# Rows of two expert layers turned inside their expert stages instead of in stages of their own

## The reference, cut to what matters

```
# L0: every token goes to its top 2 of 8 experts, each expert takes 512 rows per choice
xe = jnp.where(valid[..., None], xf[tok_idx], 0.0)
h  = jax.nn.gelu(jnp.einsum('ech,ehf->ecf', xe, w1), approximate=True)   # 256 -> 1024
ye = jnp.einsum('ecf,efh->ech', h, w2)                                   # 1024 -> 256
# L1: gated experts: silu(x @ w_gate) * (x @ w_up) @ w_down, 8 experts, inner width 352, top 2
```

## Time and profile before

| | us |
|---|---|
| median of 3 runs (3170.32 to 3171.92) | 3170.71 |
| the profiled execution, its own time | 3168.09 |
| its span, first to last instruction | 3166.2 |
| TensorE busy, 21348 matmuls | 2538.6 (80%) |
| VectorE busy | 2188.5 (69%) |
| ScalarE busy | 1274.6 (40%) |

### The profile page before, as it was taken

The page is one execution under the profiler, slowest core; times in us unless marked ns, Lnnn a source line. Parts: engine busy times, 40 slices in busy tenths (PEclk is TensorE's granted clock), DMA queues, the critical chain, the costliest instruction groups (busy, mean ns, idle before and its releaser), DMA issues. The chain is left out here.

```text
span 3166.2 us, 57355 instructions
## 1 busy us (share of the span) xinstructions
PE 2538.6 (80%) x21348; PEld 1656.4 (52%) x21348; DVE 2188.5 (69%) x5562; ACT 1274.6 (40%) x2273; POOL 990.4 (31%) x1412
## 2 busy tenths in 40 slices
PE   1998385999904497997989876886699999969982
PEld 1443263666604266886556543444466555656662
DVE  5997763666557764675678767997766545867757
ACT  1777353333202323111346654773222222256622
POOL 3442271110074260113656326871300000024330
PEclk9999598999956698998999997998799999979996
DMA  3331266221150147665721022100100000011001
GB/s 96 131 110 69 96 232 204 80 79 62 41 158 12 65 168 259 226 229 183 233 79 48 12 74 81 43 23 5 64 10 13 1 1 1 1 39 48 29 10 58
DMA packets 158167, 266.90 MB, mean 84 GB/s; under 512 B 22635, under 2 KB 106137, under 8 KB 151876
## 3 DMA queue, kind: packets, MB, share of 16 engines
q1 hardware_dynamic: 131204, 186.97, 17.8%
q0 software_dynamic: 17904, 76.23, 7.1%
q10 hardware_dynamic: 8784, 0.04, 0.2%
HBM read 175.25 MB, written 88.34 MB: 83 GB/s over the span
## 5 line engine op out<-in xcount | busy, mean ns | idle before, releaser
L1495 ACT ACTIVATE l2e_hf<-l2e_H 128x512 f32<-128x512 f32 x208 | 124.2, 597 | 381.4 <-PE l2e_H L1451 381.4
L1626 POOL TENSOR_TENSOR all_m_rstd<-all_m_sq,all_mhalf 128x8 f32<-128x8 f32 x24 | 39.6, 1648 | 557.4 <-DVE all_m_sq L1611 523.0
L772 DVE TENSOR_REDUCE l0a_mx<-l0a_S 128x2 f16<-128x512 f32 x256 | 168.0, 686 | 21.7 <-PE l0a_S L606 21.0
L1533 DVE CAST l2e_hh<-l2e_hf 128x512 f16<-128x512 f32 x208 | 92.7, 446 | 122.9 <-ACT l2e_hf L1495 108.6
L721 ACT ACTIVATE l0a_pf<-l0a_ST 128x512 f32<-128x512 f32 x256 | 146.6, 602 | 53.1 <-PE l0a_ST L620 52.9
L768 DVE CUSTOM_DVE_ANT_0 l2s_masked<-l2s_S,l2s_mq 128x128 f32<-128x128 f32 (+1 forms) x512 | 153.3, 349 | 20.4 <-PE l2s_S L606 19.9
L1451 PE MATMUL l2e_H<-l2o_hi,l2e_w 128*128 128x512 f16 x576 | 151.4, 381 | 15.8 <-DVE l2e_w L1509 15.8
L1495 ACT ACTIVATE l0e_hf<-l0e_H 128x512 f32<-128x512 f32 x128 | 76.4, 597 | 206.1 <-PE l0e_H L1451 206.1
L1451 PE MATMUL l2e_H<-l2e_hh,l2e_w 128*128 128x512 f16 x640 | 155.1, 379 | 0.0
L1535 DVE TENSOR_TENSOR l2e_hl<-l2e_hf,l2e_hh 128x512 f16<-128x512 f32 x208 | 147.3, 708 | 7.2
L1451 PE MATMUL l1e_H<-l1b_hi,l1e_w 128*128 128x256 f16 (+1 forms) x936 | 144.8, 274 | 7.8 <-DMA l1e_w<-packed,all_second_weight_row 7.8
(11 more groups left out here) (711 smaller groups left out, 7508.3 us busy)
## 6 DMA issues: line engine op xcount, KB each, us to landing
l0e_wf<-in_L_ffn_w SPq DMA_DIRECT2D x16, 1024.0 KB, 7.7
rows<-l0a_zeros SPq DMA_DIRECT2D x16, 640.0 KB, 5.9
l1u_rb<-rows SPq DMA_DIRECT2D x20, 512.0 KB, 5.0
results<-l1e_y SPq DMA_DIRECT2D x39, 256.0 KB, 3.4
l0a_kv<-in_ctx SPq DMA_DIRECT2D x16, 512.0 KB, 4.1
rows<-l0a_zeros SPq DMA_DIRECT2D x16, 512.0 KB, 4.9
l0d_p_cx<-in_ctx SPq DMA_DIRECT2D x16, 512.0 KB, 6.4
l0u_rb<-rows SPq DMA_DIRECT2D x16, 512.0 KB, 5.1
```

Of the source, the lines that this page charges most:

```text
L772: m = nc.vector.tensor_reduce(mx[h % 2][:, :, i], ps[:, :].rearrange("p (u k) -> p u k", u=TB), AX.X, ALU.max)
L1495: nc.scalar.activation(hf[q % 4][0:fn, :], pair_of(q, lay)[0][0:fn, :], lay.func, scale=1.0 / WS).then_inc(acted, 1)
L1533: nc.vector.tensor_copy(high, v).then_inc(hi_done, 1)
L1626: self.nc.gpsimd.tensor_tensor(out=(self.rstd, self.rstd2)[which][:, g], in0=(self.sq, self.sq2)[which][:, g], in1=self.g.mhalf[:, 0:self. ...
```

## The change

`turn_rows_stage` is gone, and so are `hi` and `lo` of all rows. `experts_stage` gets `raw=rows` and does the turning itself:

- SyncE loads a block of rows (512 rows in L0, 256 in L1) into a ring of 4 (L0) or 6 (L1) buffers `rb`. In L0 the loads stand around `load(n)`; in L1 six are issued first, and one behind each store.
- TensorE turns blocks 0 and 1 before the first unit. After up(a=1) it turns the next pair's first block, after down(a=0) the next pair's second. A turn is 16 transposes in L0 (two halves of 8) and 8 in L1.
- Both parts go into one of two PSUM banks `T`. ScalarE copies a half (128x1024 fp16) to `xT[b % 2]` by one instruction; VectorE copies nothing. The up unit waits for `copied`.
- The banks for `T` come from `Y`: in L0 four tiles now share two banks, so that a down tile waits for the copy 2 tiles back (`DEPTH` = 2). L1 had two `Y` banks before.

```diff
+    HALVES, BLKS = gt // 2, NE * tiles // gt
+    RING = 4 if packed is None else 6
+    DEPTH = gt if raw is None else 2
...
+            pairs = [st.ps(f"Y{i}") for i in range(2)]
+            Y = [pairs[u % 2][:, u // 2 * D:(u // 2 + 1) * D] for u in range(gt)]
+            T = [st.ps(f"T{i}", [P, 2, KD, 2, P], F16) for i in range(2)]
+            rb = [st.sb(f"rb{i}", [P, gt, 2 * D], F16) for i in range(RING)]
+            xT = [st.sb(f"xT{i}", [P, 2, KD, gn], F16) for i in range(2)]
...
                 for n in range(NE):
                     if packed is None:
+                        load_rows(2 * n)
                         load(n)
+                        load_rows(2 * n + 1)
+                    elif n == 0:
+                        for b in range(RING):
+                            load_rows(b)
...
                     if rows_out is not None and n:
                         store(n - 1)
+                        if packed is not None:
+                            load_rows(n - 1 + RING)
...
+            def next_block(un):
+                if raw is None or (un.l, un.a) not in ((0, 1), (1, 0)):
+                    return BLKS
+                first = 2 * un.n if packed is None else un.n // 2 * 2
+                return first + (2 if un.l == 0 else 3)
...
+                def turn(b):
+                    if raw is None or b >= BLKS:
+                        return
+                    pe.wait_ge(rows_in[b % RING], (b // RING + 1) * 16)
+                    for j in range(HALVES):
+                        h = b * HALVES + j
+                        if h >= 2:
+                            pe.wait_ge(copied, h - 1)
+                        for r in range(2):
+                            for k in range(KD):
+                                for u in range(2):
+                                    m = pe.transpose(T[h % 2][:, r, k, u, :],
+                                                     rb[b % RING][:, 2 * j + u, r * D + k * P:r * D + (k + 1) * P],
+                                                     ident_h[:, :])
+                        m.then_inc(turned, 1)
...
+                turn(0)
+                turn(1)
                 for un in plan:
...
+                        if raw is not None:
+                            b = 2 * un.n + a if packed is None else un.n
+                            pe.wait_ge(copied, (b + 1) * HALVES)
...
-                            if t >= gt:
-                                pe.wait_ge(added, t - gt + 1)
+                            if t >= DEPTH:
+                                pe.wait_ge(added, t - DEPTH + 1)
...
+                    turn(next_block(un))
...
+                copy(0)
                 for k in of_expert[0]:
                     convert(k)
+                copy(1)
...
+                    copy(next_block(un))
...
-def turn_rows_stage(nc, g, name, rows, n_rows, hi, lo):
```

More of the change, by code:

```diff
@@ L1299, in experts_stage @@
         H = st.ps("H", [P, 4, 512])
-        Y = [st.ps(f"Y{i}") for i in range(gt)]
+        if raw is None:
+            Y = [st.ps(f"Y{i}") for i in range(gt)]
+        else:
+            pairs = [st.ps(f"Y{i}") for i in range(2)]
[3 more added lines that the diff above has]
+            xT = [st.sb(f"xT{i}", [P, 2, KD, gn], F16) for i in range(2)]
+            ident_h = st.sb("ident_h", [P, P], F16)
+            rows_in = [st.sem(f"rows_in{i}") for i in range(RING)]
+            ident_set, turned, copied = st.sem("ident_set"), st.sem("turned"), st.sem("copied")
         w_in = [st.sem(f"w_in{i}") for i in range(NSTG)]
@@ L1433, in _ @@
                         col = (un.i * 2 + a) * gn if packed is None else 0
-                        col += un.n * tiles * P if rows_out is not None else 0
+                        if raw is not None:
+                            b = 2 * un.n + a if packed is None else un.n
+                            pe.wait_ge(copied, (b + 1) * HALVES)
                         for f, (f0, fn) in enumerate(lay.chunks):
@@ L1448, in _ @@
                                             X = (hh if x_hi else hl)[a][(un.l - 1) % n_hbuf][0:kn, k, :]
+                                        elif raw is not None:
+                                            X = xT[a][:, 0 if x_hi else 1, k, :]
                                         else:
@@ L1481, in convert, with copy @@
                                          ).then_inc(w_hi, 1)
+                def copy(b):
+                    if raw is None or b >= BLKS:
+                        return
+                    for j in range(HALVES):
+                        h = b * HALVES + j
+                        act.wait_ge(turned, h + 1)
+                        nc.scalar.activation(xT[b % 2][:, :, :, j * 2 * P:(j + 1) * 2 * P],
+                                             T[h % 2][:, :, :, :, :].rearrange("p r k u q -> p r k (u q)"), ACT.Copy
+                                             ).then_inc(copied, 1)
+                copy(0)
                 for k in of_expert[0]:
                     convert(k)
+                copy(1)
                 if send is not None:
@@ L2431, in _ @@
                 depool.on_tensor(pe)
-def turn_rows_stage(nc, g, name, rows, n_rows, hi, lo):
[L2436 to L2486, removed]
-                    nc.vector.tensor_copy(lo[:, :, n * LT * P:(n + 1) * LT * P],
-                                          ps[n % 4][1][:, :, :, :].rearrange("p k u q -> p k (u q)")
-                                          ).then_inc(lo_done, 1)
@@ L2855, in gated_layer @@
                           pack=Pack(nc, g.packed, GATED_MATS, gated_weights(io), E1 // 2, E1 // 2))
-    with Stage(nc, "l1b") as places:
-        hi, lo = places.sb("hi", [P, KD, n_rows], F16), places.sb("lo", [P, KD, n_rows], F16)
-        turn_rows_stage(nc, g, "l1u", rows, n_rows, hi, lo)
-        ex = Expert([Layer(D, F1, ACT.Silu, gated=True)], 0, [None] * 3)
-        experts_stage(nc, g, "l1e", hi, lo, to.weight_row, [ex] * (BLOCKS - 1),
-                      rows_out=results, packed=g.packed)
+    ex = Expert([Layer(D, F1, ACT.Silu, gated=True)], 0, [None] * 3)
+    experts_stage(nc, g, "l1e", None, None, to.weight_row, [ex] * (BLOCKS - 1), rows_out=results, packed=g.packed,
+                  raw=rows)
     return results
```

23 lines of the change are left out of this document (15 added, 8 removed).

## The result

| | before | after |
|---|---|---|
| median, us | 3170.52 | 3126.26 |
| runs | 4, 3167.71 to 3171.92 | 4, 3122.92 to 3127.36 |
| the profiled execution, its own time | 3168.09 | 3127.36 |
| its span | 3166.2 | 3125.6 |

The ratio is 0.986, 95% interval 0.9843 to 0.9877: 44 us faster, with an interval of 39 to 50 us. The forecast was 3132.0, a gain of 38.7. From profile to profile it is 40.7 us.

What follows compares the result with a forecast made beforehand. DMA row transfers bound the turn stages, TensorE the expert stages. -69.0 + 4.9 + 12.7 + 2.5 + 10.2 = -38.7 us from the profiled 3168.09 gives 3129.4; with the median 2.6 above, 3132.0 us, range 3124 to 3151.

Steps and rivals of the forecast that it cites:

- best bounds: Likeliest case with L0's start 3.2 us and L1's start 2.3 us cheaper than forecast: a gain of 44.2 us.
- Part 1: The turn stages of L0 and L1 disappear: 31.1 and 37.9 us, together 69.0 us saved.
- Part 2: Start of L0's expert stage: TensorE waits for block 1 behind both weight transfers and turns it, +4.9 us.
- Part 3: L0's expert stage: 14 batches of 16 transposes on TensorE at 0.91 us each, nothing absorbed, +12.7 us.
- All the covers: L0's turns: row loads, bank `T`, `xT`, ScalarE's copies and `DEPTH` 2 should cause TensorE no added wait, zero cost.
- Part 4: Start of L1's expert stage: six row loads share the DMA with the first weight gather, +2.5 us, between +0.2 and +5.0.
- the Trainium skill's rule on taking the queues in turn: Start of L1: DMA engines alternate queues packet by packet, so the gather shares with equal row bytes, an estimate of 3.6 us.
- Part 5: L1's expert stage: 37 batches of 8 cost 16.9 us, the wait before down(second) absorbs 6.7, +10.2 us.
- The sum: Whole kernel: savings and costs in L0 and L1 add to -38.7 us, giving a median of 3132.0 us.
- the low clock at the turns: Rival for both expert stages: batches run at the low clock, 32.5 us more, a gain of 6 us, 3165; 4%.
- the clock falling behind them: Rival for both expert stages: matmuls behind each of 51 turns run slow, 76 us more, 3208; 3%.
- The late gathers of L1: Rival for L1's expert stage: row loads delay weight gathers, each of 19 pairs waits 1 us, gain 20, 3151; 7%.

Runs made afterwards that it cites:

- the two-bank run: Kernel before the change, with the four tiles of an L0 down unit in two `Y` banks; L0 took 335.1 us steady, as before.
- the cut-down runs: Changed kernel with one or both of an L1 pair's batches cut from 8 transposes to 1; a pair took 12.34 us (either cut) or 12.14 (both).
- the doubled transposes: Changed kernel with every transpose done twice; an L0 batch of 32 took 1.79 us, an L1 pair 13.63, both stages at clock 1.00.

## Why the prediction was right

The forecast was 3132.0 us and the range 3124 to 3151; 3126.3 lies in it, but 2 us from its edge. The gain by the medians, 44.3 us, is just beyond the 44.2 at which all terms stood at their best bounds, so the number is met by luck in part; the steps are met better than the number. By the steps of the prediction:

- **Part 1, what goes: right.** The two turn stages are gone from the timeline. What follows them begins where they began.
- **Part 2, the start of L0: the mechanism right, the term a fourth too large.** 14.0 us forecast, 12.75 measured, +3.7 instead of +4.9. TensorE waited for block 1 as described. Its transposes began 11.1 us after the first transfer, not 12.1, and the batch took 1.67 and not 1.9 us. I had priced a block at 1.7 us from the mean rate of the turn stage; the two blocks cost (11.1 - 8.7) / 2 = 1.2 us each. In the eight traces with this start it took 12.6 to 13.2 us.
- **Part 3, the turns in L0: right.** 0.90 us a batch against 0.91. The stage grew by 12.1 us, not 12.7; some 0.5 of the difference is the clock at the start, since before, TensorE ran about 3 us at half rate and now 2. All the covers held: no wait for `copied`, `rows_in` or `Y`, and the two-bank run shows the last of them by itself.
- **Part 4, the start of L1: right in the number, by luck in part.** 8.2 us against 8.3; eight traces have 7.9 to 9.5. The middle between the bounds was a choice. Of the 2.4 us that the start really costs, 1.35 are the gather's longer way from issue to matmul beside the row loads, as I had said, where I had 2.5; the other 1.04 are its later issue, which I had left out, 0.35 of them POOL's identity copy. By the Trainium skill's rule on taking the queues in turn (DMA: Bandwidth & Descriptors, Queues, rings and completion order) my estimate was 3.6 us. That is more than any trace shows: the gather took 1.1 to 2.7 us longer from issue to matmul than the mean of 5.7 without row loads.
- **Part 5, the turns in L1: right in mechanism and size of a pair, one term mis-sized.** 12.7 us forecast, 12.73 measured, and the cut-down runs show that the wait before down(second) absorbs 0.30 us of a pair, whether it is a wait for `Y` or for the split. I had 0.35: I had priced the down matmuls at the up matmuls' 0.109 us, while 18 of them take 1.99 us (1256.68 to 1258.67), 0.111 each. The layer as a whole grew by 11.3 instead of 10.2 us. 18 pairs at 0.59 and a last one with a single batch (0.14) make 10.8, and the clock the rest: it stayed at 0.50 for some 4 us behind the first up matmul where it had 3 before, which is 0.5 us.
- **The sum.** Forecast -38.7, the two layers' stretches give -39.5, the profiled executions -40.7, the medians -44.3 with an interval of 39 to 50. That -38.7 and -39.5 lie so near is errors that cancel: L0's start cost 1.2 us less than forecast, L1's turns 1.1 more. Some 2 of the last 4 us are the one trace of the kernel before that forecast and table go by, whose layers were the shortest of three; by the means of all kept traces the layers give -41.7. The rest belongs to no step; in the traces of the two kernels some 3 us lie behind L1 (1694.7 and 1691.4), cause open.

The rivals: the low clock at the turns and the clock falling behind them are excluded by the changed kernel's own windows at 1.00 and by the doubled transposes. The late gathers of L1 did not come: from issue to landing they took 8.5 us at the median and 12.6 at most, 7.8 and 11.2 before, within the 14.4 us of slack.

## What to carry to other kernels

A stage that a transfer bounds is worth merging into one that TensorE bounds, and the price is the pitch of what moves, 0.056 us a transpose here, not the duration its row shows, 0.219. Look for a wait that recurs in each round on the engine that gets the work: what is put ahead of it is free up to its length, if it stands behind the work from which that wait runs (here both places behind up(second); that one ahead of it would move VectorE's row too is argued from the order of the work, no run tried it). The start of a merged stage is a term of its own, and a single trace does not measure it: here the same start differed by 0.6 us in L0 and 1.6 in L1 from one trace to the next, and the time at the low clock behind it by more.

## What was not expected of the hardware

- How long TensorE stays at the 1.2 GHz level at the start of a stage differs from one execution to the next. Behind the first up matmul of L0 it was at granted 0.50 for 1.0 to 2.6 us in eight traces with the same code there, for 4.1 and 1.1 us in two with an earlier start, and for 2.9, 3.0 and 5.9 us in three with the turn stage ahead. Two microseconds more of it cost one (348.2 us steady against 347.2). An earlier start of 2.3 us was worth 1.2 in one trace, one of 2.6 us 2.9 in another.
- The chips differ on the same program. On the third one the changed kernel takes 3210.9 us and not 3126.3, and the kernel before is slower by as much. The difference lies between L0 and L1: from L0's last copy to L1's first load 318 us on the one, 396 on the third. There, in the shared expert of L1, while POOL scatters rows for most of the time, TensorE pauses between single matmuls, seven times for 2.4 us and twice for 12.1 among shorter ones, for nothing the profile names:

```profile
PE l1s_Y L1528 <- issue: 56.8, 21, 12.1
```

The traces of the chip with 3252.82 us have it too, 46 to 57 us; where the changed kernel takes 3126.3 us TensorE has no such wait in that stretch. The cause stays open; no run was aimed at it.
